# Gated attention and expert feed-forward on one core: GpSimd as a staged engine, and every down product in split form

## The reference

```python
def attn(ctx, lat):                     # two heads of 64; ctx has 96 features
    xn, ln = layernorm(ctx), layernorm(lat)
    q = ln @ Wq.T
    k, v = split(concat([xn @ Wkv.T, ln @ Wlkv.T]))      # 512 keys
    a = softmax(where(mask, rmsnorm(q) * s @ rmsnorm(k).T, -big))
    return (a @ v) @ Wo.T + bo
def ffn(x):
    gates = sigmoid(x @ expert_sel.T)   # 32 experts, the 4 largest of a token count
    scores = relu(einsum('nd,edf->nef', x, keys)) * gates_of_top_4
    return einsum('nef,efv->nv', scores, values)
x = x + tanh(g_xattn) * attn(ctx, norm(x))
x = x + tanh(g_ffn) * ffn(norm(x))
```

## Time and profile before

| | us |
|---|---|
| median of 3 runs | 115.79 (115.44 to 116.35) |
| the profiled execution | 115.75 |
| its span in the profile | 114.0 |
| PE, DVE, ACT, POOL busy in the span | 105.8, 95.0, 65.6, 16.0 |
| DMA of `bo` lands | 8.54 |
| `up 0.0` begins on PE | 62.94 |
| last matmul ends | 110.77 |

### The profile page before, as it was taken

The page is one execution under the profiler, slowest core; times in us unless marked ns, Lnnn a source line. Parts: engine busy times, 40 slices in busy tenths (PEclk is TensorE's granted clock), DMA queues, the critical chain, the costliest instruction groups (busy, mean ns, idle before and its releaser), DMA issues.

```text
span 114.0 us, 2086 instructions
## 1 busy us (share of the span) xinstructions
PE 105.8 (93%) x644; PEld 86.1 (76%) x644; DVE 95.0 (83%) x309; ACT 65.6 (58%) x148; POOL 16.0 (14%) x26
## 2 busy tenths in 40 slices
PE   4993998999999999999989999999999999999980
...
PEclk9999999999999999999999999999999999999999
...
GB/s 86 223 179 397 376 10 3 3 6 0 0 0 0 6 0 0 0 3 6 0 12 49 297 270 255 178 255 198 3 12 285 299 244 229 214 126 83 0 30 154
DMA packets 7112, 12.78 MB, mean 112 GB/s; under 512 B 894, under 2 KB 2558, under 8 KB 6847
## 3 DMA queue, kind: packets, MB, share of 16 engines
...
...
HBM read 12.00 MB, written 0.66 MB: 111 GB/s over the span
## 4 chain that ended last, share of the span: by engine, by line
PE 74%; ACT 12%; DMA 4%; DVE 3%; SPq 3%; issue 1%; DVEq 1%
PE bank L724 13%; PE bank L726 13%; PE bank L725 13%; PE bank L862 10%; PE bank L849 5%; DMA bo<-wb_in 4%; PE bank L916 3%; PE bank L754 3%; PE bank L783 3%; PE bank L794 2%; PE bank L820 2%; PE bank L847 2%; ACT cx L594 1%; ACT kT L657 1%; PE bank L887 1%
## 5 line engine op out<-in xcount | busy, mean ns | idle before, releaser
L701 ACT ACTIVATE hid_hi<-keys 128x512 fp32r<-128x512 f32 x28 | 17.4, 632 | 16.8 <-DVE keys L535 13.1
L535 DVE SCALAR_TENSOR_TENSOR keys<-bank,inT 128x512 f32<-128x512 f32 x32 | 21.2, 686 | 1.1 <-PE bank L726 0.8
L552 DVE TENSOR_TENSOR hid_lo<-keys,hid_hi 128x512 fp32r<-128x512 f32 x28 | 18.4, 686 | 0.1
L862 PE MATMUL bank<-vw,prob 128*128 128x129 f32 x128 | 15.7, 278 | 0.2 <-ACT prob L670 0.2
L862 PEld LDWEIGHTS bank<-vw,prob 128*128 128x128 f32 x128 | 14.8, 191 | 1.0 <-issue 1.0
L724 PE MATMUL bank<-xm_hi,k_lo 128*128 128x512 f32 x32 | 13.7, 427 | 0.0
L726 PE MATMUL bank<-xm_hi,k_hi 128*128 128x512 f32 x32 | 12.5, 391 | 0.0
L725 PE MATMUL bank<-xm_lo,k_hi 128*128 128x512 f32 x32 | 12.5, 390 | 0.0
L445 DVE CUSTOM_DVE_ANT_0 junk<-bank,mask_b 128x512 bf16<-128x512 f32 x16 | 10.4, 689 | 2.0 <-PE bank L820 1.8
L724 PE MATMUL bank<-hid_hi,v_lo 128*128 128x512 f32 x28 | 11.3, 402 | 0.0
L670 ACT ACTIVATE prob<-bank 128x512 f32<-128x512 f32 x16 | 8.7, 594 | 4.0 <-PE bank L849 3.8
...
## 6 DMA issues: line engine op xcount, KB each, us to landing
...
```

The lines of the kernel that those rows point to most:

```text
L535: dve.scalar_tensor_tensor(hid[:, n % 3, :], bank[H_BANK[n % len(H_BANK)]][:, :], 0.0, gated[:, n % SLOTS, :], ALU.max, ALU.mult).then_inc ...
L552: dve.tensor_tensor(hid_lo[:, m % RING, :], hid[:, n % 3, :], hid_hi[:, m % RING, :].bitcast(F32), ALU.subtract).then_inc(hid_lo_ready, 1)
L701: act.activation(hid_hi[:, m % RING, :], hid[:, n % 3, :], ACT.Copy).then_inc(hid_hi_ready, 1)
L862: last = pe.matmul(bank_of(b, OUT + t)[:, WOA * a:WOA * a + WOA], prob[:, b % 2, a, j, P * t:P * t + P], vw[:, b, j, a, :], start=(j == 0) ...
```

## The change

GpSimd gets a list of its own, POOL_ORDER. From DVE it takes the Newton steps of all three norms (with four instructions instead of three, since it has no fused form here), the tiles `xn` and `xm`, the split of `expert_sel` and the 1 + exp of the gates (`add_one`); from ACT the scaling of `bo`. It makes the low part of every fourth chunk of the feed-forward. WHOLE is 0, so all 32 down products are split ones. `turn_res` transposes x_mid straight into the accumulator as its first contribution, the gates are scaled by tanh when they are copied, and `finish` becomes a plain copy: half 0 on ACT, half 1 on DVE. ACT no longer copies the transposed x_mid. The lists of PE, DVE and ACT are new orders of the same stages; in ACT's, `norm_in 0` stands ahead of `constants 0`, and PE has 16 `warm` ahead of `turn_in 0`, not 19.

```diff
-WHOLE = 4
+POOL_SLOT = RING - 1
+WHOLE = 0
...
+    warm 13, warm 14, warm 15, turn_in 0, warm 16, warm 17, fold 0, project 0, turn_in 1, warm 18, vctx 0,
+    project 1, warm 19, warm 20, warm 21, vlat 0, warm 22, turn_in 2, vctx 1, turn_qk 0, vlat 1, warm 23,
+    turn_qk 1, row_max 0.0, vlat 2, vctx 2, row_max 0.1, row_max 1.0, turn_in 3, project 2, turn_max 0, vlat 3,
+    vctx 3, row_max 1.1, weights 0.0, project 3, turn_max 1, turn_qk 2, weights 0.1, weights 1.0, row_max 2.0,
...
+    row_max 3.1, attend 1.0, attend 1.1, turn_max 3, turn_mid 0, weights 2.1, weights 3.0, select 0, attend 2.0,
+    turn_mid 1, weights 3.1, select 1, turn_gates 0, attend 2.1, turn_gates 1, attend 3.0, attend 3.1,
+    turn_mid 2, up 0.0, turn_res 0, up 0.1, up 0.2, up 0.3, select 2, up 0.4, turn_res 1, up 0.5, turn_mid 3,
+    up 0.6, down 0.0, down 0.1, down 0.2, up 0.7, down 0.3, up 0.8, down 0.4, up 0.9, up 0.10, down 0.5,
+    down 0.6, select 3, up 0.11, up 0.12, down 0.7, up 0.13, turn_gates 2, turn_gates 3, down 0.8, down 0.9,
...
+    down 0.15, turn_res 3, up 1.3, up 1.4, down 1.0, down 1.1, up 1.5, up 1.6, up 1.7, down 1.2, up 1.8,
+    down 1.3, down 1.4, up 1.9, down 1.5, up 1.10, down 1.6, down 1.7, up 1.11, down 1.8, up 1.12, down 1.9,
+    up 1.13, up 1.14, up 1.15, down 1.10, down 1.11, down 1.12, down 1.13, down 1.14, down 1.15
...
+POOL_ORDER = """
+    norm_in 0, split_sel 0, norm_in 1, scale_bo 0, mask 0, norm_in 2, newton_qk 0, newton_qk 1, norm_in 3,
+    add_bias 0, newton_qk 2, newton_qk 3, low_keys 0, low_values 0, low_keys 1, add_bias 1, low_keys 2,
+    low_values 1, norm_mid 0, low_keys 3, norm_mid 1, add_one 0, add_one 1, norm_mid 2, norm_mid 3, split 0.3,
+    add_one 2, split 0.7, low_values 2, add_one 3, split 0.11, low_values 3, split 0.15, split 1.3, split 1.7,
+    split 1.11, split 1.15
+"""
...
+    stats_in 0, scale_gq 0, stats_in 1, scale_wo 0, stats_in 2, sum_qk 0, stats_in 3, sum_qk 1, norm_qk 0,
+    norm_qk 1, row_max 0.0, row_max 0.1, row_max 1.0, turn_max 0, sum_qk 2, row_max 1.1, norm_qk 2, turn_max 1,
...
+    out_proj 3, stats_mid 3, turn_mid 2, up 0.0, up 0.1, up 0.2, split 0.0, split 0.1, up 0.3, split 0.2, up 0.4,
+    up 0.5, select 2, split 0.4, up 0.6, split 0.5, up 0.7, split 0.6, up 0.8, turn_mid 3, up 0.9, up 0.10,
+    select 3, split 0.8, split 0.9, up 0.11, up 0.12, split 0.10, up 0.13, up 0.14, split 0.12, up 0.15,
...
+    stats_in 0, norm_in 0, constants 0, stats_in 1, turn_in 0, fold 0, norm_in 1, project 0, turn_in 1,
+    stats_in 2, vctx 0, project 1, sum_qk 0, norm_in 2, stats_in 3, vlat 0, sum_qk 1, turn_in 2, turn_qk 0,
+    round_qk 0, vlat 1, turn_qk 1, round_qk 1, norm_in 3, vlat 2, vctx 1, vctx 2, turn_in 3, project 2, vlat 3,
...
+    split 0.0, split 0.1, split_values 2, split 0.2, turn_mid 3, split 0.3, split 0.4, select 2, split 0.5,
+    split 0.6, split 0.7, split 0.8, split 0.9, split_values 3, select 3, split 0.10, turn_gates 2, turn_gates 3,
...
+    split 1.13, finish 0, split 1.14, split 1.15
...
+        def acc(b):
+            return bank[ACC_BANK[b // HB]][:, S * (b % HB):S * (b % HB) + S]
+
+        def wait_low(engine, m):
+
+            if m % RING == POOL_SLOT:
+                engine.wait_ge(pool_lo_ready, m // RING + 1)
+            else:
+                engine.wait_ge(hid_lo_ready, m + 1 - (m + 1) // RING)
...
+            def newton(y, v, w):
+
+                then(pool.tensor_tensor(w[:, 1, :], y, y, ALU.mult))
+                then(pool.tensor_tensor(w[:, 2, :], w[:, 1, :], v, ALU.mult))
+                then(pool.tensor_scalar(w[:, 1, :], w[:, 2, :], -0.5, 1.5, ALU.mult, ALU.add))
+                return pool.tensor_tensor(w[:, 3, :], w[:, 1, :], y, ALU.mult)
+
+            def mask(i):
+                pool.wait_ge(in_mask, 16)
+                pool.tensor_scalar(mask_b[:, :, 0:S], mask_u8[:, :, :], BIG, -BIG, ALU.mult, ALU.add).then_inc(mask_ready, 1)
+
+            def norm_in(b):
+                pool.wait_ge(var_ready, b + 1)
+                pool.tensor_scalar(nm_in[:, b, :], mv_in[:, b, BT:, 0], -1.0, None, ALU.mult)
+                pool.wait_ge(y0_in, b + 1)
+                then(newton(rs_in[:, b, 0, :], var_in[:, b, :], rs_in[:, b, :, :]))
+                pool.tensor_tensor(nb_in[:, b, :], nm_in[:, b, :], rs_in[:, b, 3, BT:], ALU.mult).then_inc(nb_ready, 1)
+                for t in range(BT):
+                    j = BT * b + t
+                    pool.tensor_scalar(xn[:, j, :], x[:, j, :], mv_in[:, b, t, 0:1],
+                                       rs_in[:, b, 3, t:t + 1], ALU.subtract, ALU.mult).then_inc(xn_ready, 1)
+
+            def newton_qk(b):
+                pool.wait_ge(ms_ready, b + 1)
+                pool.wait_ge(y0_qk, b + 1)
+                newton(rs_qk[:, b, 0, :], ms[:, b, :], rs_qk[:, b, :, :]).then_inc(rs_qk_ready, 1)
...
+            def norm_mid(b):
+                pool.wait_ge(var_mid_ready, BT * (b + 1))
+                pool.tensor_scalar(var_mid[:, b, :], mv_mid[:, b, :, 1], LN_EPS, None, ALU.add)
+                pool.wait_ge(y0_mid, b + 1)
+                then(newton(rs_mid[:, b, 0, :], var_mid[:, b, :], rs_mid[:, b, :, :]))
+                for t in range(BT):
+                    j = BT * b + t
+                    pool.tensor_scalar(xm[:, j, :], x_mid[:, j, :], mv_mid[:, b, t, 0:1],
+                                       rs_mid[:, b, 3, t:t + 1], ALU.subtract, ALU.mult).then_inc(xm_ready, 1)
+
+            def split_sel(i):
+                pool.wait_ge(in_wa, 16)
+                pool.tensor_copy(sel_hi[:, :], wa[:, A_SEL:A_SEL + E]).then_inc(sel_ready, 1)
+                pool.wait_ge(sel_ready, 1)
+                pool.tensor_tensor(sel_lo[:, :], wa[:, A_SEL:A_SEL + E], sel_hi[:, :].bitcast(F32),
+                                   ALU.subtract).then_inc(sel_ready, 1)
+
+            def add_one(b):
+                t = slice(BT * b, BT * b + BT)
+                pool.wait_ge(exp_ready, b + 1)
+                pool.tensor_scalar(one_e[:, t, :], exp_l[:, t, :], 1.0, None, ALU.add).then_inc(one_ready, 1)
+
+            def low_part(q, src, hi, lo, hi_ready, lo_ready):
+                part = slice(QUARTER * q, QUARTER * (q + 1))
+                pool.wait_ge(hi_ready, q + 1)
+                pool.tensor_tensor(lo[:, part], src[:, part], hi[:, part].bitcast(F32), ALU.subtract).then_inc(lo_ready, 1)
+
+            def split(h, c):
+                n = EC * h + c
+                m = n - WHOLE
+                pool.wait_ge(hid_ready, n + 1)
+                pool.wait_ge(hid_hi_ready, m + 1)
+                if m >= RING:
+                    pool.wait_ge(down_done, n - RING + 1)
+                pool.tensor_tensor(hid_lo[:, m % RING, :], hid[:, n % 3, :], hid_hi[:, m % RING, :].bitcast(F32),
+                                   ALU.subtract).then_inc(pool_lo_ready, 1)
+
+            def scale_bo(i):
+                pool.wait_ge(in_bo, 16)
+                pool.wait_ge(tanh_ready, 1)
+                pool.tensor_scalar(bo[:, :], bo[:, :], tanh_g[:, 0:1], None, ALU.mult).then_inc(bo_ready, 1)
...
+                dve.wait_ge(one_ready, b + 1)
...
+                dve.wait_ge(down_done, EC * (h + 1))
                 for b in range(HB * h, HB * h + HB):
-                    dve.wait_ge(midT_ready, b + 1)
-                    dve.wait_ge(down_done, EC * (h + 1))
-                    dve.scalar_tensor_tensor(res[:, b, :], bank[ACC_BANK[h]][:, S * (b % HB):S * (b % HB) + S],
-                                             tanh_g[:, 1:2], x_midT[:, b, :], ALU.mult, ALU.add).then_inc(res_ready, 1)
-
-            run = {"stats_in": stats_in, "norm_in": norm_in, "sum_qk": sum_qk, "norm_qk": norm_qk,
+                    dve.tensor_copy(res[:, b, :], acc(b)).then_inc(res_ready, 1)
...
-                act.wait_ge(in_bo, 16)
-                act.activation(bo[:, :], bo[:, :], ACT.Copy, scale=tanh_g[:, 0:1]).then_inc(bo_ready, 1)
...
-                act.activation(gateT[:, b, :], bank_of(b, TURN_GATES)[0:E, 0:S], ACT.Copy).then_inc(gateT_ready, 1)
+                act.activation(gateT[:, b, :], bank_of(b, TURN_GATES)[0:E, 0:S], ACT.Copy,
+                               scale=tanh_g[0:E, 1:2]).then_inc(gateT_ready, 1)
...
+            def finish(h):
+                act.wait_ge(down_done, EC * (h + 1))
+                for b in range(HB * h, HB * h + HB):
+                    act.activation(res[:, b, :], acc(b), ACT.Copy).then_inc(res_act_ready, 1)
...
-                                     start=(c == 0), stop=(c == EC - 1))
+                                     start=False, stop=(c == EC - 1))
...
-                    pe.wait_ge(hid_lo_ready, m + 1)
+                    wait_low(pe, m)
                     last = product(bank[ACC_BANK[h]][:, :], (v_hi[:, cc], v_lo[:, cc]),
-                                   (hid_hi[:, m % RING, :], hid_lo[:, m % RING, :]), c == 0, c == EC - 1)
+                                   (hid_hi[:, m % RING, :], hid_lo[:, m % RING, :]), False, c == EC - 1)
...
```

(33 more changed lines are left out.)

128 lines of the change are left out of this document (41 added, 87 removed).

## The result

The changed kernel takes 117.36 us (117.32 to 117.66, 4 runs) against 116.07 for the one before on the same chip (4 runs): ratio 1.0119, 95% interval 1.0061 to 1.0177. It is slower by about 1.3 us where 2.3 us of gain were forecast. The profiled execution took 117.34, its span is 115.5 us.

A forecast was written before the change was run, and what follows sets the result against it. From about 12 us PE's own list, or how early it starts, was taken to set the end. Start -1.8, feed-forward -0.4, the rest 0 gave -2.2: span 111.8, with 1.75 outside it 113.5 us, range 112.8 to 114.3.

The forecast's parts named there:

- Part 1: The start: without ACT's wait for bo and with POOL's Newton step, the lead is 1.8 us.
- rival B: POOL's small steps cost 0.4 to 0.5 us with hand-over; net -1.0, 114.8 us, no tellable change; chance 0.13.
- Part 4: Front and attention: DVE relieved -0.3, ACT's extra splits +0.3; nothing, with 0.5 us either way.
- Most of these have an `attend` in front of them: Longer chains through POOL mostly stand behind an attend of 1.9 or 3.7 us on PE; -0.1 to +0.5.
- At about 43.5 it is free: POOL's queue: five low parts and a bias addition, 7.6 us from about 35, finish when norm_mid 0's root comes.
- Part 2 and 3: Feed-forward: plain products become split ones, -0.7, PE waits 0.3, net -0.4; POOL's low parts hidden, 0.1 at the end, cancelled.
- always the later: Feed-forward up to down 0.11: PE, at 0.69 us an item, is always later than DVE, at 0.6.
- C: POOL and DVE block each other in the feed-forward, deciding above about 4 us lost; up to 117.1 us; chance 0.08.
- D: The lists fit the new durations badly, queue heads wait in several places, the gain is spent; 115.5 us; chance 0.07.

The follow-up runs named there:

- e7: Kernel before with the start part alone: bo scaled on POOL, ACT's norm_in 0 ahead of the constants, 16 warms; 116.39 us, ratio 1.0061.
- e9: Kernel before up to its first up product, then the changed kernel's whole feed-forward with its lists; 116.26 us, ratio 1.0058.
- e11: e9 plus two unused 32-byte SBUF tensors where the changed kernel has them; 116.75 us, ratio 1.0097.
- e14: Kernel before with the residual part alone: residual transposed into the accumulator, scaled gates, plain copies at the end; 115.74 us, ratio 1.0000.
- e15: e14 with every fourth hidden low part (seven) on POOL, plain products kept; 116.35 us, ratio 1.0076.
- e3: Changed kernel with the xn and xm tiles back on DVE, Newton steps still on POOL; 116.88 us, ratio 1.0148.
- e6: e3 with the second norm's Newton steps and add_one also back on DVE; 116.05 us, ratio 1.0031.
- e10: e6 with POOL starting its last key low part only when xm of sequence 0 is written; 115.27 us, ratio 0.9974.
- e1: Changed kernel with only the eight xm tiles back on DVE, Newton steps still on POOL; 117.39 us, ratio 1.0182.
- e16: Changed kernel with its two new small tensors allocated last, nothing else; 117.07 us, ratio 1.0140.

## Why the prediction was wrong

**Part 1** gave 1.8 us and 1.72 were there at `attend 1.1`. Its steps were less good than its sum. The small POOL steps were right (0.20, one each 0.28, for 0.22), so rival B fell. `xn` at 0.29 a tile was taken from a select and is 0.79. `project 0` came at 9.79, not 9.2, and ACT's second `turn_in` ended at 13.4, not 12.5. And the reason was half a reason: the chain named `bo`, the last of two waits, and behind it stands `nb_in`, in other executions the later one (e7 has the numbers). The baseline was also a late draw: five executions with the front of before (before, e9, e11, e14, e15) scale `bo` at 8.57, 7.58, 7.65, 8.70 and 7.77 and have `project 0` at 11.23, 10.67, 10.90, 11.37 and 10.73. Against the mean of these, 10.98, the lead is 1.2. In all of them but before, the mask held DVE's Newton step or `nb_in` by 0.7 to 0.9 us.

**Part 4** is the step that failed: "nothing, with 0.5 either way". Attention became 3.5 us longer (16.54 to 20.05). Taken back one after the other, the tiles give 1.1 (e3), Newton steps and `add_one` 1.4 (e6), and the last key low part moved out of DVE's way 0.7 (e10); 0.3 is left of e10 against before, the new order. The 0.7 is no cost of the changed kernel, in whose attention no DVE instruction is held by POOL. That collision came in with the tiles on DVE (e1, e3, e6), and hid some of what they gave back. What is shown is the sum: tiles, Newton steps and `add_one` on POOL cost 3.2 of the 3.5 us. How the 3.2 divide between slow steps and POOL's queue (`norm_mid 0` and `add_one 0`, each behind other work) no run separates. I had argued from DVE's load, which was not full. But `norm_mid` is a chain of latencies between PE's stages. To move a link of it to a slower engine lengthens the chain however idle the first one was. "Most of these have an `attend` in front of them" was not checked stage by stage: the chain after runs over POOL at `turn_mid` 0, 1 and 2, so the cover was used up at each. "At about 43.5 it is free" was 45.12, while the root was there at 44.58; 35 and 7.6 make 42.6 in the first place, POOL's first low part began at 36.13, and a wait of 1.5 for ACT's high part was not in the sum.

**Part 2 and 3.** -0.4 for the FFN against -0.23 in the changed kernel looks like a hit and is not one. Run from an `up 0.0` in time, this FFN (with `norm_mid 3` on DVE) costs 1.0 more than before (e9), and it is short in the changed kernel only because late PE finds DVE's first chunks ready. The 0.7 saved on plain products was real as PE work and was filled with holes: e9 loses 0.4 at `up 0.3` and 0.8 at `up 0.6`, by the distance from one start to the next, where I had 0.3 in all. Between `up 0.1` and `up 0.3` DVE there has `norm_mid 3` and two low parts (65.55 to 68.45); PE was not "always the later". POOL's low parts were not free: 0.6, not 0.1. The 0.6 was the upper end that I gave, for 1.76 us at the very end; there it was 0.4 with a low part of 1.29. The wider matmul spacing, 0.2 us of FFN (e9 and e11, after and e16), was in no term.

**Rivals.** C named a mechanism that exists, and the right direction, but not the cause: in the changed kernel two DVE instructions of the FFN are held by POOL, 0.75 us together where C needed 4, and none in attention. The block of 1.04 us on a four-column conversion is e6's. That the time came near C's 117.1 is luck. D, lists that fit badly, holds 0.3 us by order, and what POOL's queue cost in attention besides. No rival held what happened most, a chain longer by slower links. The chance for slower, 0.08, was too small. For the changed kernel, then, the slower links are shown as a whole and their shares are open.

**Open.** Not tried: what of the 0.3 us left in attention is which list entry; POOL's list in another order with the norms still on it; `bo` taken from ACT with the constants left in place; the refinement of the first root early on DVE.
